# Two samples in one gram matmul, and a copy by ScalarE between the gram and VectorE's turn

## What is computed

```python
all_vecs = jnp.concatenate([dense_proj[:, None, :], sparse_embs], axis=1)   # 2048, 27, 128
interactions = jnp.einsum('bnd,bmd->bnm', all_vecs, all_vecs)
rows, cols = np.triu_indices(n, k=1)
z = jnp.concatenate([dense_proj, interactions[:, rows, cols]], axis=1)
h = jnp.concatenate([z, r_dense_proj], axis=1)                               # 2048, 607
h = jnp.maximum(h @ W_top1 + b_top1, 0.0)                                    # 512
h = jnp.maximum(h @ W_top2 + b_top2, 0.0)                                    # 256
y = h @ W_top3
```

## Time and profile before

| | before |
|---|---|
| device time, median of 3 runs | 374.51 us (373.56 to 376.5) |
| the profiled execution's own time | 371.39 us |
| its span in the trace | 369.6 us |
| TensorE: matmul, weight load | 91%, 84% of the span |
| VectorE, ScalarE, GpSimd | 66%, 38%, 67% |
| granted TensorE clock, mean | 0.99 |

### The profile page before, as it was taken

The page is one execution under the profiler, slowest core; times in us unless marked ns, Lnnn a source line. Parts: engine busy times, 40 slices in busy tenths (PEclk is TensorE's granted clock), DMA queues, the critical chain, the costliest instruction groups (busy, mean ns, idle before and its releaser), DMA issues.

```text
span 369.6 us, 14433 instructions
## 1 busy us (share of the span) xinstructions
PE 334.6 (91%) x6192; PEld 310.2 (84%) x6192; DVE 244.6 (66%) x702; ACT 138.8 (38%) x232; POOL 245.9 (67%) x260
## 2 busy tenths in 40 slices
PE   0766789999899899999999999999999999998986
PEld 0665789989798898989899898989899898997775
DVE  4999998989465684659667694659667694611110
ACT  2246332536043250435334260435324260435322
POOL 5877777777777777777777777777777777720000
PEclk9998999999999899999999999999999999999999
DMA  6999943242244211531244211532244211300000
GB/s 192 276 265 245 284 134 124 57 126 52 59 150 124 59 50 50 156 121 52 55 116 153 58 50 50 156 121 50 57 132 138 57 50 50 85 21 4 18 2 0
DMA packets 16758, 36.94 MB, mean 100 GB/s; under 512 B 5661, under 2 KB 8733, under 8 KB 16735
## 3 DMA queue, kind: packets, MB, share of 16 engines
q1 hardware_dynamic: 8479, 19.80, 17.9%
q0 software_dynamic: 8192, 16.79, 17.3%
q10 hardware_dynamic: 64, 0.01, 0.0%
HBM read 36.57 MB, written 0.01 MB: 99 GB/s over the span
## 4 chain that ended last, share of the span: by engine, by line
PE 84%; DVE 6%; DMA 3%; issue 3%; SPq 2%; ACT 1%
PE gram L418 14%; PE hid L384 13%; PE look_odd L338 8%; PE look_odd L340 8%; PE look_ps L338 7%; PE look_ps L340 7%; PE vec_act L311 7%; PE hid L392 7%; DVE onehot L572 4%; PE hid L338 4%; PE hid L340 4%; DMA raw<-tbl 3%; DVE look_lo L580 2%; PE small L353 1%; SPq L245 1%
## 5 line engine op out<-in xcount | busy, mean ns | idle before, releaser
L292 POOL DMA_INDIRECT vecs<-tbl,ids_sb x256 | 245.7, 960 | 80.0 <-issue 77.5
L572 DVE TENSOR_SCALAR onehot<-step_ids,row_no 125x256 fp32r<-125x256 int32 x640 | 202.4, 387 | 43.1 <-PE look_odd L340 23.0
L547 ACT COPY vecs_T<-vec_act 128x512 f32<-128x512 f32 x64 | 46.0, 731 | 78.2 <-PE vec_act L311 78.2
L338 PE MATMUL look_odd<-onehot,look_hi 125*128 125x256 f32 x256 | 69.6, 306 | 5.4 <-DVE look_lo L580 5.4
L338 PE MATMUL look_ps<-onehot,look_hi 125*128 125x256 f32 x256 | 67.2, 299 | 4.7 <-DVE look_lo L580 2.9
L340 PE MATMUL look_odd<-onehot,look_lo 125*128 125x256 f32 x256 | 63.9, 284 | 0.0
L340 PE MATMUL look_ps<-onehot,look_lo 125*128 125x256 f32 x256 | 63.8, 285 | 0.0
L418 PE MATMUL gram<-vecs_T 128*27 128x26 f32 x4096 | 52.3, 193 | 9.6 <-issue 5.3
L418 PEld LDWEIGHTS gram<-vecs_T 128*27 128x27 f32 x4096 | 43.7, 104 | 18.9 <-issue 15.7
L338 PEld LDWEIGHTS look_odd<-onehot,look_hi 125*128 125x128 f32 x256 | 49.0, 191 | 7.3 <-DVE look_lo L580 6.2
L338 PEld LDWEIGHTS look_ps<-onehot,look_hi 125*128 125x128 f32 x256 | 49.4, 193 | 5.6 <-DVE look_lo L580 5.3
(11 more groups left out here) (70 smaller groups left out, 275.7 us busy)
## 6 DMA issues: line engine op xcount, KB each, us to landing
step_ids<-look_ids SPq DMA_DIRECT2D x15, 640.0 KB
raw<-tbl SPq DMA_DIRECT2D x10, 448.0 KB
vecs<-tbl,ids_sb POOLq DMA_INDIRECT x256
dense_new<-dense SPq DMA_DIRECT2D x8, 128.0 KB
dense_T<-dense SPq DMA_DIRECT2D x8, 128.0 KB, 2.3
raw<-tbl SPq DMA_DIRECT2D x10, 52.0 KB
step_ids<-look_ids SPq DMA_DIRECT2D x1, 512.0 KB
w_sb<-w SPq DMA_DIRECT2D x1, 512.0 KB
```

What stands on the lines that cost most here:

```text
L292: nc.gpsimd.indirect_dma_start(out=vecs[j][:, k, :], out_offset=None, in_=tables[k], in_offset=bass.IndirectOffsetOnAxis(ap=ids_sb[:, t, k ...
L338: nc.tensor.matmul(bank, look_hi[:, f, ch, :], onehot[:, i % SLOTS, c, :], start=ch == 0, stop=False)
L547: return engine_copy(vecs_T[j][:, :, lo:lo + GROUP], bank[:, :, :].rearrange("d v b -> d b v"))
L572: last = nc.vector.tensor_scalar(onehot[:, i % SLOTS, c, :], step_ids[a][0:LOOK_K, f - a * LOOKUPS // 2, :], row_no[0:LOOK_K, ch:ch + 1], ...
```

## The change

- **Gram matmuls.** One matmul takes two neighbouring samples: 64 columns of weights (2 x 32 places of `vecs_T`) and 52 streamed columns (2 x 26), in two column groups of 64. Of its 64 x 52 results the two blocks of a sample with itself are wanted, the two of one sample with the other are not. A tile has 64 such matmuls (128 records), in two pieces of 32 (`gram_half`, 64 records each).
- **Padding.** `vecs_T` has 32 places a sample instead of 28; the five unused ones are set to zero at the start by two more VectorE memsets.
- **A copy in between.** ScalarE copies the wanted blocks of each piece from PSUM to `gram_sb` in SBUF (`save_gram`, four copies of 32 partitions x 416 elements a piece). VectorE's `turn` waits for `gram_saved` of both pieces and reads `gram_sb`.
- **Order.** TensorE's first piece stands behind unit 4 and `pairs_out`, the second one behind unit 9, at the end of the tile. `pairs_out` moves from behind unit 1 to behind unit 4. ScalarE's `copy_pairs` moves with it.
- **The rest.** The MLP's sample order is permuted to fit (`dense_mlp`, an array of the same size); `gram_sb` and `mask` lie in buffers of the raw tables, and the mask's load stands later in SyncE's queue.

```diff
-ROW = 28
-HALF = ROW // 2
+ROW = 32
+HALF = 14
+HALF_SLOTS = QUAD // 2
+BANK_SLOTS = HALF_SLOTS // 2
+SLOT = 4 * FOLD
...
+        gram_sb = raw[1][:, P:P + QUAD * 2 * FOLD].rearrange("p (g n) -> p g n", g=QUAD)
-        gram = psum("gram", [P, QUAD, QUAD])
+        gram = psum("gram", [P, 2, 512])
...
-                def gram_part(j, part):
-                    for g in range(GRAM_PARTS[part], GRAM_PARTS[part + 1]):
-                        for s in range(P // QUAD):
-                            v = vecs_T[j][:, s * QUAD + g, :]
+                def gram_half(j, half):
+                    rows = vecs_T[j].rearrange("d b v -> d (b v)")
+                    wanted = vecs_T[j][:, :, 0:2 * HALF].rearrange("d b (h n) -> d b h n", h=2)
+                    for n in range(half * HALF_SLOTS, (half + 1) * HALF_SLOTS):
+                        lo = n % BANK_SLOTS * SLOT
+                        bank = gram[:, n % HALF_SLOTS // BANK_SLOTS, lo:lo + SLOT]
+                        for g in range(2):
+                            b = (g * QUAD + n) * 2
                             last = nc.tensor.matmul(
-                                gram[s * QUAD:s * QUAD + VECS, g, 0:2 * FOLD], v[:, 0:VECS],
-                                v.rearrange("d (h n) -> d h n", h=2)[:, :, 0:FOLD], start=True, stop=True)
-                    return last
+                                bank[g * 2 * QUAD:(g + 1) * 2 * QUAD, :], rows[:, b * ROW:(b + 2) * ROW],
+                                wanted[:, b:b + 2, :, 0:FOLD], start=True, stop=True)
+                    last.then_inc(gram_ready, 1)
...
                     if positive(t):
-                        pe.wait_ge(gram_turned, t)
+                        pe.wait_ge(gram_saved, 2 * t)
...
-                def gram_second(j):
-                    gram_part(j, 2)
-                    gram_part(j, 3).then_inc(gram_ready, 1)
+                def gram_second(t, j):
+                    pe.wait_ge(gram_saved, 2 * t + 1)
+                    gram_half(j, 1)
...
                 def turn(t):
-                    dve.wait_ge(gram_ready, t + 1)
+                    dve.wait_ge(gram_saved, 2 * t + 2)
+                    if positive(t):
+                        dve.wait_ge(folded, t)
                     nc.vector.transpose(gram_rows[:, :, :, :].rearrange("p h n m -> p (h n m)"),
-                                        gram[:, :, 0:2 * FOLD].rearrange("p g n -> p n g")).then_inc(gram_turned, 1)
+                                        gram_sb[:, :, :].rearrange("p g n -> p n g")).then_inc(gram_turned, 1)
...
+                def save_gram(t, half):
+                    act.wait_ge(gram_ready, 2 * t + half + 1)
+                    if half == 0 and positive(t):
+                        act.wait_ge(gram_turned, t)
+                    slots = gram[:, :, 0:BANK_SLOTS * SLOT].rearrange("p b (k s n) -> p b k s n", k=BANK_SLOTS, s=2)
+                    kept = gram_sb[:, half * HALF_SLOTS:(half + 1) * HALF_SLOTS, :].rearrange(
+                        "p (b k) n -> p b k n", b=2)
+                    for s in range(4):
+                        rows = slice(s * QUAD, (s + 1) * QUAD)
+                        last = nc.scalar.copy(kept[rows], slots[rows, :, :, s % 2, :])
+                    last.then_inc(gram_saved, 1)
```

More of the change, by code:

```diff
@@ L71 @@
 EARLY = 4
-PARTS = 4
-GRAM_PARTS = tuple(QUAD * n // PARTS for n in range(PARTS + 1))
+HALF_SLOTS = QUAD // 2
+BANK_SLOTS = HALF_SLOTS // 2
+SLOT = 4 * FOLD
 H1, H2 = 512, 256
@@ L88, in pair_rows, with build @@
     return np.array(rows)
-def build(nc, dense_rows, ids, look_ids, tables, look_tables, w1_dense, w1_pairs, b1, w2, b2, w3,
+def build(nc, dense_rows, dense_mlp, ids, look_ids, tables, look_tables, w1_dense, w1_pairs, b1, w2, b2, w3,
           fold_mask, identity, row_numbers, out):
@@ L459, in tile @@
                     turn_group(n, k, 1)
-                    if not first:
-                        pairs_out(t - 1, j, pair)
                     unit(2)
@@ L464, in tile @@
                     unit(4)
-                    if not mlp:
-                        gram_first(t, j, pair)
+                    if not first:
+                        pairs_out(t - 1, j, pair)
+                    gram_first(t, j, pair)
                     if mlp and j == 1:
@@ L477, in tile @@
                     unit(8)
[L478 to L480 removed]
+                    unit(9)
+                    gram_second(t, j)
                     if mlp and j == 1:
                         layer3(pair - 1)
[L483 to L487 removed]
+                pe.wait_ge(dve_set, 5)
                 for i in range(LOOKUPS):
@@ L719, in tile @@
                     copy(n, k, 1)
-                    if not first:
-                        copy_pairs(t - 1, 1 - j)
                     place_dense(n, k, pair + j)
@@ L728, in tile @@
                     unit(3)
+                    if not first:
+                        copy_pairs(t - 1, 1 - j)
+                    save_gram(t, 0)
                     copy(n, k, 2)
@@ L739, in tile @@
                     unit(9)
+                    save_gram(t, 1)
                     if mlp and j == 1:
@@ L773, in _ @@
                 last = tiles - 1
-                copy_pairs(last - 2, 1)
                 merge(1, pairs - 1, True)
@@ L777, in _ @@
                 place_dense(last, 1, pairs - 1)
+                save_gram(last - 1, 0)
+                copy_pairs(last - 2, 1)
                 relu1(pairs - 2, 0)
+                save_gram(last - 1, 1)
                 for q in range(GROUPS):
@@ L781, in _ @@
                 relu1(pairs - 2, 1)
+                save_gram(last, 0)
                 copy_pairs(last - 1, 0, pairs_end)
+                save_gram(last, 1)
                 relu2(pairs - 2)
@@ L810 @@
         "dense": dense,
+        "dense_mlp": np.ascontiguousarray(dense.reshape(D, -1, 2, QUAD, 2).transpose(0, 1, 2, 4, 3).reshape(D, -1)),
         "ids": np.ascontiguousarray(ids[:, large].reshape(-1, P, GATHERS).transpose(1, 0, 2)),
@@ L832 @@
     out = nc.dram_tensor("y", (dense.shape[1] * Y_PARTS // (2 * P), 2 * P // Y_PARTS), F32, kind="ExternalOutput").ap()
-    build(nc, ap["dense"], ap["ids"], ap["look_ids"], [ap[f"tbl_{f}"] for f in large],
+    build(nc, ap["dense"], ap["dense_mlp"], ap["ids"], ap["look_ids"], [ap[f"tbl_{f}"] for f in large],
           [ap[f"tbl_{f}"] for f in small], ap["w1_dense"], ap["w1_pairs"], ap["b1"], ap["w2"], ap["b2"],
@@ L836 @@
     r = run_bass_kernel_spmd(nc, [arrays], core_ids=[0])
-    return np.ascontiguousarray(r.results[0]["y"]).reshape(dense.shape[1], 1)
+    return np.ascontiguousarray(r.results[0]["y"].reshape(-1, 2, 2, QUAD).transpose(0, 1, 3, 2)).reshape(dense.shape[1], 1)
```

40 lines of the change are left out of this document (17 added, 23 removed).

## The result

The changed kernel takes 397.17 us (median of 4 runs, 395.69 to 398.18) against 374.03 us before (4 runs, 372.92 to 376.5): a ratio of 1.067, with a 95% interval of 1.063 to 1.071. That is 23.1 us slower, where 16 were forecast. The profiled execution has a span of 395.3 us, 25.7 more than before.

The account below looks back on a forecast made before the run. TensorE was taken to set the time from about 50 us on, its gram blocks held up by instruction delivery. Terms 4.3 + 2.3 + 6.0 + 3.5 = +16 us on the 374.51 us median gave 390.5; range 377 to 400, own range 384 to 397.

Parts of the forecast that it names:

- The sign: Whole kernel: slower by over 1%, chance 0.83; within 1% 0.08, faster by over 1% 0.09.
- the rival with the long copy chain: Strided copies take longer, unit 4 stalls 1.7 us or more in each such tile: 399 to 400 us; chance 0.13.
- Term 1: Gram blocks: records 29.5 ns apart, set by the weight load, pieces of 1.98 us; +4.3 us.
- Streaming: Rival, gram blocks: loads hide behind 52 streamed columns, 23 ns a record; 377.5 us, 372.4 at the low end; chance 0.15.
- delivery: Rival, gram blocks: instructions are what is paid, 14.4 ns a record whatever its size; 357 us; chance 0.06.
- no overlap: Rival, gram blocks: the two column groups don't overlap, 58 ns a record, +74 us; 448 us; chance 0.04.
- Term 2: Between gram blocks and look-ups: 12 more blocks, 0.19 us each for changes of form; +2.3 us (1 to 4).
- Term 3: Unit 4: the copy chain makes it late, TensorE stalls 0.8 us in loop tiles with j = 0; +6.0 us (3 to 13).
- Term 4: Behind the loop: nothing covers ScalarE's copies, so TensorE waits; +3.5 us (1.5 to 5.5).
- the rival of 357 us: Gram blocks: a record costs 14.4 ns whatever its size, so half as many gain 18 us; chance 0.06.

Follow-up runs that it names:

- e10: The changed kernel with e9's two edits and one sample a gram matmul again, in two pieces of 128 records a tile: 383.38 us, ratio 1.033 to before.
- e9: The changed kernel with unit 4's one-hot columns made ahead of VectorE's turn and ScalarE's other order behind the loop: 385.22 us, ratio 1.038 to before.
- e12: The changed kernel as it is, run again on the same chip as e9, e10 and e11: 396.87 us, ratio 1.071 to before.
- e2_unit4_ahead: The changed kernel with five units' one-hot columns instead of four made ahead of VectorE's turn: ratio 1.049 to before.
- e11: The changed kernel with 13 unused float32 matmuls where TensorE waits for ScalarE behind the loop: 393.88 us against 396.87; ratio 1.063 to before.
- e3_end_order: The changed kernel with ScalarE's pair copy and first save ahead of the merges behind the loop, two turned groups ahead of the second save: ratio 1.053 to before.
- e7: The kernel before with only the padding to 32 places a sample, two more memsets and the mask's later load: ratio 1.000 to before.
- e1_one_sample: The changed kernel with the gram matmul of before (one sample, 27 columns of weights, four column groups), pieces of 128 records: ratio 1.058 to before.
- e6: The kernel before with its gram matmuls in four blocks of 64 records behind units 5 to 8, tiles up to 13: ratio 0.996 to before.
- e8: The changed kernel with unit 4's columns ahead of the turn, ScalarE's other order behind the loop, and layer 3 ahead of the second piece: ratio 1.037 to before.
- e4: The changed kernel with gram_sb laid out so that VectorE's transpose reads neighbouring words and ScalarE writes strided ones: ratio 1.112 to before.

## Why the prediction was right, and where it was wrong

The sign came true, and the total only in part: 397.17 us is 6.7 above the 390.5 of the sum, just outside the forecast's own range of 384 to 397. It is nearer to the 399 to 400 us of the rival with the long copy chain, but not by that rival's mechanism: the stall at unit 4 was 0.65 us in the loop, not 1.7. What the sum lacked lies mostly behind the loop and at the branch.

**Term 1, the gram blocks: right.** Records come 29.4 ns apart in all 32 pieces but the one at half clock, and a piece takes 2.005 us; 29.5 and 1.98 were forecast, from the weight load of 64 columns at 0.85 ns and a handover of the size that today's records have. Streaming (23 ns), delivery (14.4) and no overlap (58) are all excluded as the size of a record. That the load sets it is read from the fit: 29.4 ns in two groups are 58.8 ns in each, 54 of load and 5 of handover. No run varied the columns of weights and the streamed ones apart. The chain from e10 to e9 gives the price in the loop without the rest: 0.80 us a lap, 0.20 a piece. The Trainium skill's TensorEngine Tiling, Instruction Overhead, counts some 60 cycles for any matmul with up to 60 streamed columns. The records of 7.5 ns alone don't speak against that, since with four groups they are 30 ns in each; but the new ones are 58.8 ns in each of two groups with 52 streamed columns, and a fixed cost would have been the same for both. So the trace doesn't bear the rule out, and the rival built on it falls.

**Term 2, changes of form: right, and one thing was left out.** e10_two_mended_one has the gram matmuls of before, in four pieces instead of two blocks a lap, and no stall at unit 4. Its lap is 0.85 us longer than before. Two more changes at 0.19 are 0.38, and the loop's branch is 0.46: from layer 3's last record to the next look-up it is 0.61 us, against 0.15 when unit 9 follows. I listed unit 9 as moved and asked only how much time it had covered for unit 4's chain, not for the branch. Five laps, 2.3 us. (The gram's own time in a lap is 7.1 us there against 7.0 before; such sums are good to 0.2 or 0.3 us a lap.)

**The lap in sum.** 41.68 before; 0.85 for form and branch (e10); 0.80 for the records (e9 against e10); 0.72 for unit 4 (e12 against e9): 44.05. These are differences between measured laps, so they must add up; what they give is each part's size. I had expected 43.3.

**Term 3, unit 4: the size right, its parts not.** 6.0 us were forecast, e2_unit4_ahead took away 6.5 to 7. In the chain behind T (213.34 us) ScalarE starts at 0.27 (0.3 forecast) and saves in 2.02 us (1.67): four copies of 32 partitions start 0.51 us apart and don't overlap, as the copies of 128 partitions seemed to the earlier trace rows. VectorE starts at once (0.03, forecast 0.55), and from its transpose to the one-hot columns it takes 2.81 us (2.11), since a strided source in SBUF costs 1.82 us. With 1.27 that gives T + 6.40 instead of 5.95; and TensorE, held up by the branch, would be there at T + 5.75 instead of 5.19 (its record ahead starts at 218.97 us, and 0.12 us is the usual step). That is 0.65 us of stall, and the step behind it is 0.22 us instead of 0.12: 0.75 against 0.8. The errors cancel, which is luck. I had kept 1.05 us for the transpose, with only a shorter one in mind.

**Term 4, the end: failed.** 3.5 us were forecast, all of it waits. The part behind the last layer 3 of the loop is 11.0 us longer, and since it lost unit 9 (1.0 us), 12.0 have to be named. The slower pieces are 2.5 of them (0.6, 0.8, 0.8 and 0.25, at full clock), which belong to term 1. Half clock is 3.4 (e11), and I had nothing for it: three waits of 1.9 to 2.1 us each are followed by 3.4 us at half clock, and before the change the waits there were 1.08 and 0.57. The rest, 6.1 us, are waits where the term had 3.5. Layer 1 starts at T + 8.65 instead of the 7.2 of the sum: between the first save and the merges ScalarE also copies the result of layer 3 and issues its DMA (L688, L690: 347.74 to 348.84, 1.1 us), which I didn't list, and each save is 0.35 longer. Tile 15's vectors come 1.5 late, not 1.1. And the last save isn't hidden: `pairs_out` waits 1.0 us more for VectorE's fold (381.92). By e3_end_order, a better order saves 6.2 us, its part of the clock included.

**The start.** The first gram record comes 1.3 us later than before (53.76 against 52.49 us). Tiles 1 and 2 stall by 1.6 and 1.5 us at unit 4, where 0.85 and 1.16 were forecast. In return the change does gain here: the gram blocks up to the first layer 3 take 16.0 us instead of 19.0, since those before were held up most by delivery (4.90 and 5.16 us for the two of the first lap). One unit 9 more (1.0) lies in this part. Padding and memsets are no cause of the 1.3 us (e7), and it isn't the same each time: e1_one_sample, whose program is the same up to the first gram matmul, starts it at 52.55 us, and the changed kernel's other profiled execution (e12) at 53.29. So the 1.3 us isn't shown to belong to the change.

**The whole.** By the terms, measured (forecast): the pieces 32 x 2.005 - 58.96 = 5.2 us (4.3); changes of form 2.3 (2.3); the branch 2.3 (0); unit 4 6.7 (6.0); the end without its pieces 9.5 (3.5); a later start 1.3 (0). That is 27.3 against 25.7 measured and 16 forecast; without the start it is 26.0, and sums like this one are not exact to the last 1 or 2 us. The step that failed is term 4, by 6 us; the branch is the second, by 2.3.

## What to carry to other kernels

Before a matmul is made larger to save instructions, compare the array's time for it with the time in which the instructions of the small one arrive: here 29.4 against some 14 ns a record, with only half as many records. Where blocks wait for instructions, spreading them between longer matmuls removes part of the wait without a slower record, but here its changes of form ate most of the gain (e6: 0.4%). When work moves away from a place, ask for everything that it stood in front of: a branch, a chain on another engine, a wait behind the loop; and list what else the waited-for engine issues there.

## What was not expected of the hardware

- **Half clock behind short waits.** In the changed kernel waits of about 2 us on TensorE are followed by 3.4 us at the 1.2 GHz level, and work without use in them takes time away (e11: 3.0 us). It isn't the same each time: e3, e8 and e9 have ScalarE's same order behind the loop, with none, 6.8 + 3.4 us and 3.4 us of half clock, and e8 varies from one execution to the next. The kernel before isn't free of it: in its profiled execution 3.4 us at half clock follow a gram block in which TensorE waited 1.3 us for instructions (a window of 123 to 127 us has 0.57). What decides is open.
- **Strides.** A transpose of 832 words a partition takes 1.05 us from a dense source in SBUF (e4) and 1.82 from a strided one there, but 1.05 from a strided one in PSUM; ScalarE's copy of 416 words a partition takes 0.50 us to neighbouring words and 0.89 to strided ones.
- **GpSimd is close behind TensorE.** I read its 67% as room. A view of the gathers before shows their first and last start:

```profile
L292 POOL DMA_INDIRECT vecs<-tbl,ids_sb x256: 941/947/1651, 2.7 to 325.2; - x128
```

256 gathers in 322.5 us are 1.26 each, with 0.3 us for "issue" between them and next to no wait for another engine. 32 of them, a lap's worth, take 40.3 us, and the lap before takes 41.68. So, if a gather can't come sooner than that, at most some 1.4 us a lap were to be had from TensorE in the steady loop, and the rival of 357 us could not have been reached in it. This is an estimate from the row; no run tests it.
